# Placing the score steps of the next head group 0.03 of a group's work earlier in a fused attention and expert kernel

## The reference, cut to what matters

```python
scores = jnp.einsum('bhqd,bhkd->bhqk', q, k) / math.sqrt(HD)
scores = jnp.where(causal, scores, -jnp.inf)
attn = jax.nn.softmax(scores, axis=-1)
out = jnp.einsum('bhqk,bhkd->bqhd', attn, v)
...
h = x + attention(rmsnorm(x, ln1_w), ...)
out = h + moe(rmsnorm(h, ln2_w), ...)
```

## Time and profile before

| what | value |
|---|---|
| time, median of 3 executions | 2440.21 us (2437.26 to 2441.37) |
| the profiled execution's own time | 2441.37 us |
| its span in the profile | 2439.5 us |
| TensorE (PE) busy | 2199.1 us, 90% |
| VectorE (DVE) busy | 1509.0 us, 62% |
| ScalarE (ACT) busy | 1091.3 us, 45% |
| GpSimd (POOL) busy | 1063.8 us, 44% |
| mean granted clock of TensorE | 0.962 of full speed |

### The profile page before, as it was taken

The page is one execution under the profiler, slowest core; times in us unless marked ns, Lnnn a source line. Parts: engine busy times, 40 slices in busy tenths (PEclk is TensorE's granted clock), DMA queues, the critical chain, the costliest instruction groups (busy, mean ns, idle before and its releaser), DMA issues. The chain is left out here.

```text
span 2439.5 us, 38146 instructions
## 1 busy us (share of the span) xinstructions
PE 2199.1 (90%) x12944; PEld 1506.5 (62%) x12944; DVE 1509.0 (62%) x4192; ACT 1091.3 (45%) x2214; POOL 1063.8 (44%) x1092
## 2 busy tenths in 40 slices
PE   6898989999898999988999998898488899999993
PEld 4665555666556566655656666463266688888872
DVE  3666667666676765667666665664365556556557
ACT  1335554333555433454543345444233355555543
POOL 1456454444564443555443464544045133333323
PEclk9999999999999999999999999997799899999997
DMA  5434555443455444444544535333547687788796
GB/s 178 114 110 117 142 148 158 127 122 105 126 144 172 121 133 113 123 146 118 163 122 138 149 115 147 79 87 104 181 165 281 213 200 188 200 212 194 190 274 226
DMA packets 221390, 374.83 MB, mean 154 GB/s; under 512 B 24846, under 2 KB 95374, under 8 KB 218382
## 3 DMA queue, kind: packets, MB, share of 16 engines
q1 hardware_dynamic: 157454, 272.69, 38.0%
q0 software_dynamic: 17792, 39.99, 8.4%
q10 hardware_dynamic: 45952, 59.71, 6.8%
HBM read 126.88 MB, written 144.24 MB: 111 GB/s over the span
## 5 line engine op out<-in xcount | busy, mean ns | idle before, releaser
L646 ACT ACTIVATE probs<-scoresT 128x512 f32<-128x512 f32 (+3 forms) x1024 | 426.6, 438 | 512.2 <-PE scoresT L1031 499.3
L827 DVE CUSTOM_DVE_ANT_0 unused<-score,mask 128x128 bf16<-128x128 f32 (+3 forms) x1024 | 468.8, 486 | 271.6 <-PE score L1008 257.8
L1031 PE MATMUL scoresT<-stacks 97*128 97x256 f32 (+2 forms) x1024 | 421.6, 430 | 21.1 <-ACT probs L646 9.3
L1008 PE MATMUL score<-stacks 96*128 96x256 f32 (+2 forms) x1024 | 391.3, 428 | 36.7 <-DVE rowmax L827 35.9
L579 POOL TENSOR_TENSOR probs<-probs 128x1536 f32<-128x1536 f32 (+1 forms) x128 | 373.0, 2914 | 29.4 <-PE out_ps L1045 20.6
L1008 PEld LDWEIGHTS score<-stacks 96*128 96x128 f32 x1024 | 182.2, 191 | 201.6 <-issue 150.4
L840 DVE RECIPROCAL total<-total 128x128 f32<-128x128 f32 x256 | 232.7, 932 | 95.1 <-ACT whole L657 89.7
L568 POOL TENSOR_SCALAR_AFFINE_SELECT probs<-probs 128x512 f32<-128x512 f32 x256 | 165.2, 645 | 283.7 <-ACT probs L646 283.7
L1031 PEld LDWEIGHTS scoresT<-stacks 97*128 97x128 f32 x1024 | 190.6, 191 | 149.1 <-ACT probs L646 88.8
L938 PE MATMUL middle<-wqkv,XT 128*128 128x128 f32 x2048 | 267.5, 278 | 7.0 <-ACT XT L613 6.1
L1668 POOL DMA_INDIRECT h_summed<-y,goal x88 | 141.7, 1610 | 294.2 <-ACT y L1764 274.1
(11 more groups left out here) (185 smaller groups left out, 3795.9 us busy)
## 6 DMA issues: line engine op xcount, KB each, us to landing
stacks<-parts SPq DMA_DIRECT2D x768, 128.0 KB, 2.4
x_slots<-mask ACTq DMA_DIRECT2D x56, 1032.0 KB, 4.7
xr<-x_slots SPq DMA_DIRECT2D x22, 1032.0 KB
raw<-in_gates SPq DMA_DIRECT2D x24, 512.0 KB
raw<-in_ups SPq DMA_DIRECT2D x24, 512.0 KB
raw<-in_downs SPq DMA_DIRECT2D x24, 512.0 KB
normed<-in_L_attn_x SPq DMA_DIRECT2D x8, 1024.0 KB, 8.3
rows<-in_L_attn_x SPq DMA_DIRECT2D x8, 1024.0 KB, 5.6
```

The lines of the kernel that those rows point to most:

```text
L646: act.activation(probs[j][:, h, 0:width], scoresT[:, u % ST_BANKS, first:first + width], ACT.Exp, scale=SCALE).then_inc(exp_done, 1)
L827: ins = dve.tensor_tensor_reduce(unused[:, t, 0:width], score.bank(name)[:, first:first + width], mask[:, T - width:T], 1.0, MASKED, ALU.a ...
L1008: ins = pe.matmul(score.bank(name)[:, first:first + width], heads[0:ROWMAX, 0, h, t * P:(t + 1) * P], heads[0:ROWMAX, 1, h, 0:width], star ...
L1031: pe.matmul(scoresT[:, u % ST_BANKS, 0:T - first], heads[0:ROWMAX + 1, 1, h, j * P:(j + 1) * P], heads[0:ROWMAX + 1, 0, h, first:T], start ...
```

## The change

The first number of `S_AT` goes from 0.27 to 0.24. The spacing 0.055 stays. All twelve `S` steps of every group therefore get a share smaller by 0.03: 0.24, 0.295, 0.35, ... 0.845 in the place of 0.27, 0.325, 0.38, ... 0.875. No other constant and no instruction changes.

```diff
 ST_BANKS = 2
 QUARTERED = ("P", "KR", "KU", "V", "Y", "LAT")
 T_AT = (0.9, 0.9, 0.9, 0.9)
-S_AT = (0.27, 0.055)
+S_AT = (0.24, 0.055)
 WIDE = CT * FF
```

## The result

The changed kernel takes 2467.0 us (median of 4 executions, 2466.0 to 2468.3). On the same chip the kernel before takes 2440.8 us (4 executions, 2437.3 to 2443.5). The ratio is 1.0108, 95% interval 1.0091 to 1.0127: slower by 26 us, or 1.1%. The forecast was 2435 us in a range from 2426 to 2447 us, so the time lies outside the range and on the other side. The profiled execution after took 2468.37 us with a span of 2466.6 us; against the profiled one before, its span is 27.1 us longer.

What follows compares the result with a forecast made beforehand. The prediction took TensorE to bound most groups, and VectorE, GpSimd or ScalarE to end those with long waits. Its terms summed to -5.4 us against the median 2440.21 us, giving 2435 us, range 2426 to 2447 us.

Steps and rivals of the forecast that it cites:

- Group 1: Four groups, n mod 16 = 1: fewer waits before the last quarter of `P`, 0.25 us each, 1.0 us gained.
- The rest: 0: The 36 other groups, the same work in another order: 0, bound 0.1 us each way, 3.6 us.
- Group 5: Four groups, n mod 16 = 5: `PV` 0 sets the end and comes 0.3 us later, 1.2 us lost.
- Groups 7 and 11: Eight groups, n mod 16 = 7 or 11: the wait of `S` 3.2 goes, 0.35 us each, 2.8 us gained.
- Group 13: Four groups, n mod 16 = 13: half the wait of `S` 3.2 goes, 0.8 us gained, bounds 0 and 1.8.
- Group 8: Four groups, n mod 16 = 8: `M` stops waiting, but ScalarE's negation comes no sooner, 0 gained.
- Group 9: Four groups, n mod 16 = 9: stall moves to `S` 3.2, last reduction 0.5 us sooner, 2.0 us gained.
- The ring of `ST`: Rival: `ST` steps of tiles 2 and 3 become neighbours and wait for exponentials, 2446 us; chance 0.10, 0.08 of it slower.
- the stacks: Rival: `S` 0.0 waits for late stack copies in groups 7 and 11, slower from 1.3 us late on; chance 0.05.
- something that I don't see: Rival: an unnamed cause anywhere in the kernel makes it slower, no size given; chance 0.03.

Runs made afterwards that it cites:

- LN earliest: The changed kernel with normalizations `LN` 2 and 3 of groups 17, 33 and 49 two filler quarters earlier, beside `LN` 0 and 1: 2434.7 us, ratio 1.0050.
- `S` 0.0 earlier: The changed kernel with `S` 0.0 of each group another 0.03 earlier, ahead of the last quarter of `KR`: 2434.3 us, ratio 1.0038.

## Why the prediction was wrong, step by step

- **Group 1: the step that failed most.** "Only waits before that quarter count" put down 1.0 us gained. There are 14.6 us lost. I looked at TensorE's waits and left out what VectorE does between `S` 0.1 and `S` 0.2: the normalizations fall behind the reduction of `S` 0.1, and there they meet GpSimd's first addition. The prediction's account of the order says that "VectorE's reductions move along with `S` in its queue" and looks at nothing else on VectorE; that they move past its other work is what it leaves out. I had the mechanism in hand in group 9, with its price, for an addition of two arrays, and did not ask in which other groups a VectorE instruction on arrays in SBUF is near a GpSimd one. The 0.25 us of gain had no row under it either.
- **"The rest: 0".** The 36 groups lose 13 us together, against bounds of 3.6. Most of it is in the kinds 6 and 10 (+7.9). I saw that `S` 0.2 passes `PV` 0, and took TensorE, busy all the time, as a sign that order can't matter. `PV` 0, with the filler before it, was the cover of a wait that the trace before doesn't show, because it was covered. The bound of 0.1 us each way was wrong too for 2, 3, 14 and 15: +0.2 to +0.3 in most of them, ScalarE's copy of the last quarter before `T`. Group 62, of kind 14, is 2.07 us longer at a granted clock of 0.53 against 0.73.
- **Group 5: right in kind, too small.** `PV` 0 sets the end there, as said. The term was 0.3 us each; the four groups show 1.60, 0.79, -0.05 and 1.87, together 4.2 in the place of 1.2, since `S` 0.2 brings a wait with it (0.38 us at 627.75 in group 21) and not only its own length. The 0.79 of group 21 stands at the same granted clock (0.95 in both); the groups of 1.60 and 1.87 have 0.90 in the place of 0.95, and that of -0.05 has 0.95 in the place of 0.89.
- **Groups 7 and 11.** Half right: 7 gains 0.38, 0.38, 0.38 and 0.35 us, on the 0.35 forecast, and `S` 3.2 has no wait. In 11 the four groups give 0.6 together.
- **Group 13**: 1.9 us gained, 0.8 forecast, just beyond the bound of 1.8.
- **Group 8: the wrong path.** 2.5 us gained, 0 forecast. `M` waits no more, and ScalarE's negation comes no sooner, as said (24.58 us after the group's first `ST` in group 24, before 24.48). But the next group's first `ST` does not wait for it. In the kernel before TensorE has no idle time from `M` at 713.05 to that `ST`, and its own work sets the time:

```profile
714.69 1.98 PE L1066 MATMUL middle<-wo,outT 128*128 128x512 f32 x4
716.69 0.50 PE L1031 MATMUL scoresT<-stacks 97*128 97x512 f32 x1
```

So all of what `M` gains arrives: `M` comes 0.93 us sooner after the group's start, the next `ST` 1.01.
- **Group 9**: the stall moves on to `S` 3.2, as said (2.95 us in group 25), but `S` 3.1 waits too (1.24 us). The two additions take 0.88 and 1.95 us, 0.31 less than before, and the last reduction still begins 0.12 us later in the group, where 0.5 sooner was forecast; `S` 0.2 waits 1.08 us there, where it had no wait before. The kinds 5 and 9 together fall from +7.1 to +2.9 us when `S` 0.2 goes back. For kind 9 it is +2.9 us in the place of -2.0.
- **The rivals.** The ring of `ST` and the stacks did not come as ways to be slower: `ST` waits 66.7 us, not over 94, and no `S` 0.0 waits for its stack. The case that came was the one given 0.03, "something that I don't see".
- **The division of the 26 us** is shown by runs: 14 go with the normalization (LN earliest, 1.0108 to 1.0050), and 17 with the reduction of `S` 0.0 (`S` 0.0 earlier, 1.0108 to 1.0038, of which the trace gives 7.4 to the kinds 6 and 10). They add up to 31, 5 more than the whole, and 5.8 us of gains in 7, 8 and 13 stand against them. The two repairs were not run together. In the kinds 5 and 9 the loss without the clock can be read where the granted clock is the same before and after: 0.79 us in group 21 (0.95) and 0.73 in group 25 (0.88). How the rest divides in 5, 9 and 14 between `S` 0.2 and the clock is not settled, since these groups differ from one execution to the next by as much.

## What to carry to other kernels

Before a step is moved past a neighbour in a fixed order, ask what that neighbour was covering: a wait that is hidden has no row, so it has to be worked out from when the bank or array that the step needs comes free. Look for every VectorE instruction on arrays in SBUF that slides towards a long GpSimd one, one-input ones too, and leave it room (0.38 us of lead was enough here, 0.07 was not). A shift that is good in some groups and bad in others is worth making only in the first: three kinds of sixteen gave 8 us, all sixteen cost 26.

## What the runs showed of the hardware

- A one-input normalization in SBUF (128x512) takes 0.54 us, and 3.78 us when it begins with GpSimd's addition of 3.43 us; with the addition in halves 2.17 us. It was held when it began 0.07 us before the addition by their records, and not with a lead of 0.48 us, nor of 0.38 (the first one in group 17 of the kernel with `S` 0.0 earlier, at 509.94 us, 0.54 us long, against the addition at 510.32).
- Held, it ends 0.3 us after GpSimd's instruction, whatever part of it was left: started 1.80 us behind the addition it takes 1.96 us, 1.39 behind 2.35, 0.09 behind 3.63, and 0.07 ahead 3.78. A reduction that reads PSUM takes its 0.69 us inside such an addition.
- After a wait of 3 us TensorE's granted clock can fall to half for about 4 us (0.50 from 815.1 to 819.4 us), which made two matrix products of 1.02 us 1.91 us long. It does not always: in the same execution another wait of 3.04 us, in group 12, was followed by 1.00 (392.1 to 396.4 us); after the same wait of 2.28 us in group 17 it was 0.58 in one kernel's execution and 1.00 in another's; and a wait of 1.33 us brought no fall.
